# A fused linear-attention and mixture-of-experts block on one core: third slot reordered, x's deviations behind the gate steps, x1 squared in one operation

## The reference, cut to what matters

```
x = x + conv(_ln_c(x))            # layer norm over channels, then linear attention
    k = relu(Wk x + bk); q = relu(Wq x + bq); v = Wv x + bv      # 8 heads of 8 channels
    context = k^T v over all pixels of an image (per head)
    attended = context^T q;  conv = Wr attended + br
t = tokens(x)                      # one token of 64 channels per pixel
t = t + ffn(_ln_t(t))              # layer norm, then 8 experts, top 2 by a softmax router
    out = p1 * expert[i1](t) + p2 * expert[i2](t),  p normalised over the two
```

## Time and profile before

| | |
|---|---|
| median of 3 runs | 672.26 us (671.27 to 673.7) |
| the profiled execution's own time | 671.9 us |
| its span in the trace | 670.1 us |
| mean granted TensorE clock | 0.992 of full speed |
| PE busy | 616.2 us (92%), 8318 instructions |
| DVE busy | 515.1 us (77%), 1176 instructions |
| ACT busy | 425.2 us (63%), 832 instructions |
| POOL busy | 396.1 us (59%), 350 instructions |

### The profile page before, as it was taken

The page is one execution under the profiler, slowest core; times in us unless marked ns, Lnnn a source line. Parts: engine busy times, 40 slices in busy tenths (PEclk is TensorE's granted clock), DMA queues, the critical chain, the costliest instruction groups (busy, mean ns, idle before and its releaser), DMA issues.

```text
span 670.1 us, 21498 instructions
## 1 busy us (share of the span) xinstructions
PE 616.2 (92%) x8318; PEld 276.3 (41%) x8318; DVE 515.1 (77%) x1176; ACT 425.2 (63%) x832; POOL 396.1 (59%) x350
## 2 busy tenths in 40 slices
PE   3799989779999999999999999999999999998887
PEld 1566656444444444444444444444332332332222
DVE  3534455978888888889788787987799999989844
ACT  2355545576666675766757576766766776766642
POOL 7232342237565655666666556655577777777875
PEclk9799989999999999999999999999999999999999
DMA  6223635666555566655545665554565667446542
GB/s 149 56 76 79 146 97 129 150 167 159 122 122 134 126 147 146 159 142 138 133 111 130 147 152 127 129 116 104 133 154 127 157 172 170 101 111 142 126 111 48
DMA packets 32662, 86.21 MB, mean 129 GB/s; under 512 B 7650, under 2 KB 7826, under 8 KB 32562
## 3 DMA queue, kind: packets, MB, share of 16 engines
q1 hardware_dynamic: 32082, 84.64, 52.8%
q0 software_dynamic: 288, 0.19, 0.2%
q10 hardware_dynamic: 192, 0.01, 0.0%
HBM read 34.47 MB, written 16.78 MB: 76 GB/s over the span
## 4 chain that ended last, share of the span: by engine, by line
PE 62%; DVE 18%; ACT 10%; issue 7%; DMA 1%; POOL 1%; ACTq 0%; DVEq 0%; SPq 0%; POOLq 0%
PE bank L1092 26%; PE bank L1078 7%; PE bank L1015 5%; PE bank L993 4%; PE bank L979 4%; DVE z L826 3%; PE bank L938 3%; PE bank L1089 3%; PE bank L962 3%; DVE x L731 3%; ACT grows L569 2%; DVE xnT L686 2%; PE bank L1039 2%; DVE osb L836 2%; ACT L529 2%
## 5 line engine op out<-in xcount | busy, mean ns | idle before, releaser
L442 POOL TENSOR_TENSOR z<-gbs,x1d 128x512 f32<-128x512 f32 x256 | 320.2, 1275 | 185.2 <-ACT gbs L575 72.6
L1095 PE MATMUL bank<-z,ew 128*64 128x512 f32 x512 | 243.7, 598 | 0.0
L1092 PE MATMUL bank<-z,ew 128*64 128x512 f32 x512 | 243.6, 598 | 0.0
L826 DVE TENSOR_TENSOR z<-bank,x1d 128x512 f32<-128x512 f32 x256 | 164.7, 675 | 16.2 <-PE bank L1078 16.2
L575 ACT COPY gbs<-bank 128x512 f32<-128x512 f32 x256 | 140.7, 594 | 43.8 <-PE bank L1078 41.3
L433 POOL TENSOR_TENSOR xsq<-xin 128x512 f32<-128x512 f32 x64 | 65.4, 1043 | 81.7 <-DMA xin<-in_x_dram 76.0
L1078 PE MATMUL bank<-grows,sel 64*64 64x512 f16 x1024 | 93.2, 387 | 16.3 <-ACT grows L569 7.3
L1092 PEld LDWEIGHTS bank<-z,ew 128*64 128x64 f32 x512 | 64.9, 136 | 104.6 <-issue 96.3
L503 ACT COPY xn<-bank 128x512 f32<-128x512 f32 x64 | 34.4, 589 | 62.8 <-PE bank L938 62.8
L1095 PEld LDWEIGHTS bank<-z,ew 128*64 128x64 f32 x512 | 64.7, 136 | 0.0
L686 DVE TENSOR_TENSOR xnT<-bank,rstd 128x512 f32<-128x512 f32 x64 | 41.0, 682 | 30.2 <-PE bank L924 28.5
(11 more groups left out here) (135 smaller groups left out, 804.8 us busy)
## 6 DMA issues: line engine op xcount, KB each, us to landing
x1d<-x SPq DMA_DIRECT2D x128, 256.0 KB, 4.5
xin<-in_x_dram SPq DMA_DIRECT2D x64, 256.0 KB, 4.2
x_again<-in_x_dram SPq DMA_DIRECT2D x64, 256.0 KB, 4.2
out_dram<-osb SPq DMA_DIRECT2D x128, 128.0 KB, 2.4
k<-in_const_dram SPq DMA_DIRECT2D x1, 453.5 KB, 3.8
ew_nat<-in_L_ffn_expert_w_dram POOLq DMA_DIRECT2D x2, 64.0 KB, 6.4
sel<-in_const_sel_dram SPq DMA_DIRECT2D x1, 128.0 KB, 3.4
bk_rows<-bk_wide ACTq DMA_DIRECT2D x6, 1.0 KB, 1.7
```

What stands on the lines that cost most here:

```text
L442: pool.tensor_tensor(z[:, 1, i % R_Z, :], gbs[:, i % R_Z, :], x1d[:, g % 2, 1, u * NT:(u + 1) * NT], ALU.mult).then_inc(z_pool, 1)
L826: dve.tensor_tensor(z[:, 0, i % R_Z, :], bank[:, :], x1d[:, g % 2, 0, u * NT:(u + 1) * NT], ALU.mult).then_inc(taken_of(("spread", i, 0)), 1)
L1092: pe.matmul(out_bank[0:C, :], ew[:, j, :], z[:, 0, i % R_Z, :], start=False, stop=(j == PAIRS - 1), skip_group_check=True).then_inc(prod_d ...
L1095: pe.matmul(out_bank[C:P, :], ew[:, j, :], z[:, 1, i % R_Z, :], start=False, stop=(j == PAIRS - 1), skip_group_check=True).then_inc(prod_d ...
```

## The change

It does three things, in the lists of all engines concerned. In slot 2 the order of uses becomes spread(i), queries, attended, spread(i+1), on PE and on ACT, and in the list of bank uses. In slot 3 DVE runs x's last three deviation steps behind the gate steps instead of before them. ACT squares x1 in one operation of 1024 columns, which waits for both halves of x1, and the routing rows wait for one signal per group.

```diff
@@ bank_uses
             if k == 2:
+                for i in iterations(n, k + 1)[:1]:
+                    yield from (("spread", i, s) for s in range(S))
                 if real(n - L_KEYS):
                     yield from (("queries", n - L_KEYS, s) for s in range(S))
-                for i in iterations(n, k + 1)[:1]:
-                    yield from (("spread", i, s) for s in range(S))
                 if real(n - L_ATTEND):
                     yield from (("attended", n - L_ATTEND, u) for u in range(U))
@@ ACT
-            def square_x1(g, u):
-
-                when_taken(act, ("attended", g, u))
+            def square_x1(g):
+
+                for u in range(U):
+                    when_taken(act, ("attended", g, u))
                 if g:
                     when_filled(act, ("rows", g - 1 + L_ROUTE, 0))
-                nc.scalar.activation(x1sq[:, u * NT:(u + 1) * NT], x1[:, g % R_X1, u * NT:(u + 1) * NT], ACT.Square
-                                     ).then_inc(x1_squared, 1)
+                nc.scalar.activation(x1sq[:, :], x1[:, g % R_X1, :], ACT.Square).then_inc(x1_squared, 1)
...
                     if k == 2:
+                        for i in iterations(n, k + 1)[:1]:
+                            copy_gates(i)
                         if real(n - L_KEYS):
                             for s in range(S):
                                 take_queries(n - L_KEYS, s)
-                        for i in iterations(n, k + 1)[:1]:
-                            copy_gates(i)
...
                     if k == 3:
                         if real(n - L_ATTEND):
-                            for u in range(U):
-                                square_x1(n - L_ATTEND, u)
+                            square_x1(n - L_ATTEND)
@@ DVE
-                    if k == 3 and real(n - L_COLS):
-                        x_deviations(n - L_COLS, 4, N_XSTAT)
                     for phase, (k0, k1) in gates_by_phase.items():
                         if quad_in(n, k, phase) is not None:
                             gates(quad_in(n, k, phase), k0, k1)
+                    if k == 3 and real(n - L_COLS):
+                        x_deviations(n - L_COLS, 4, N_XSTAT)
                     for i in iterations(n, k + 1)[1 if k == 2 else 0:]:
                         product(i)
@@ PE
-                    pe.wait_ge(x1_squared, (g + 1) * U)
+                    pe.wait_ge(x1_squared, g + 1)
...
                     if k == 2:
+                        for i in iterations(n, k + 1)[:1]:
+                            broadcast(i)
                         if real(n - L_KEYS):
                             make_queries(n - L_KEYS)
-                        for i in iterations(n, k + 1)[:1]:
-                            broadcast(i)
                         if real(n - L_ATTEND):
                             attend(n - L_ATTEND)
```

## The result

The changed kernel is slower: 677.36 us median of 13 runs (676.29 to 678.86) against 673.03 us of the kernel before (13 runs, 671.27 to 676.08). The ratio is 1.0066, with a 95% interval of 1.0053 to 1.0079, so 3.6 to 5.3 us, under 1% of the time. The profiled execution took 676.59 us, its span is 674.8 us.

A forecast was written before the change was run, and what follows sets the result against it. PE, busy 92% of the span, was taken as the bound, with DVE a second bound in odd steps. Savings of 5.4 + 0.9 + 0 + 0.4 = 6.7 us from 671.9 gave 665.2 us; range 660 to 675.5.

The forecast's parts named there:

- Order of slot 2, even steps: Slot 2, eight even steps 18 to 32: PE waits 0.59 us instead of 1.27, saving 0.68 us each, 5.4 us.
- The wait for one gate copy: Slot 2, even steps: PE still waits 0.59 us for one gate copy, where it waited 1.27 for two queries.
- Order of slot 2, odd steps: Slot 2, odd steps 17 to 31: last spreading 0.46 us shorter each, 3.7 us in all, if DVE allows; counted as 0.
- the second bound: Odd steps: the chain runs on DVE without a pause; if DVE stays where it is, PE arrives earlier and waits.
- If L653 is through first, only L654 is stopped. I take this value.: Slot 3, odd steps: L654 stopped until 314.34, DVE's product at about 314.3 as before, so the odd steps give 0.
- the first rival: Slot 3, odd steps: POOL stops L653 and L654 in a row, 1.2 us in eight steps, +9.6, 674.8 us; chance 0.27.
- The pair of steps: An odd and an even step together: expected 0.7 us shorter, as a sign that the forecast holds.
- the one stop: Slot 3, odd steps: only one of x's deviation steps stopped, none in the even steps; 665.2 us, chance 0.43.
- Even steps, x's steps: Slot 3, even steps: x's deviation steps meet no stop, only the gates' own L652 does; PE keeps its 0.68 us.
- Squares: ACT's square of x1: one operation saves 0.1 us each; on the chain in steps 11 to 14, 0.4 us.
- In the expectations: Forecasts written for the follow-up runs; deviations alone: no odd-step stop, 2.2 us less than before, ratio 0.997.

## Why the prediction was wrong

The forecast was 665.2 us with 0.6 on faster; the kernel came out slower, outside the range. By its own steps:

- **Order of slot 2, even steps.** Right: 0.68 us each was forecast and 0.68 is measured (19.43 to 18.75), in the changed kernel and alone. The wait for one gate copy stayed, as forecast.
- **Order of slot 2, odd steps.** Right: the piece lost 0.5 us (0.46 was forecast), and gave nothing by itself, because DVE is the second bound there. The run with the order alone shows it.
- **The step that failed: "If L653 is through first, only L654 is stopped. I take this value."** The two instants were worked out as 313.08 for L653 and 313.07 for POOL, 8.00 and 7.99 us behind the slot's start. They came out as 316.56 - 308.57 = 7.99 and 316.52 - 308.57 = 7.95. The working was right to 0.04 us and still could not say who comes first. POOL did; L653 was stopped by the first product and L654 by the second (L652 and L653 in the changed kernel's lines), which is the first rival word for word. It was priced at 1.2 us in each of eight odd steps; measured is 19.92 - 18.73 = 1.19. The pair of steps, forecast 0.7 us shorter, is 0.5 us longer (38.16 to 38.67). Between steps 17 and 34 the rival's terms come to 9.6 - 5.4 - 0.5 = 3.7 us more than before, and 3.4 are measured. The rival's 674.8 us lies 2.6 us below the measured median and 1.8 us below the profiled execution. In that execution the stretch ahead of step 17 is 1.7 us longer, 1.1 of them at the lower clock; the remainder of the median is left open.
- **Why the one stop was taken.** A tie of 0.01 us between a gain and a loss was given to the gain, 0.43 against 0.27, with no row that spoke for it. The taken case exists: in the run with the deviations alone the second step began 0.09 us ahead of POOL's pair (316.44 and 316.53), was through in 0.17 us beside it, and only the third was stopped. Which of the two cases this kernel would be was beyond the working, so a hit would have been luck. And the range ended at 675.5, 0.7 above the centre of the rival, so the rival's own spread was cut off; the measured 677.36 is that case, with the remainder on top.
- **Even steps, x's steps.** Right: none is stopped, only the gates' own first step, 1.15 us. The margin was as thin as forecast: the last of x's steps ends at 298.51 and POOL's next pair starts at 298.59.
- **Squares.** 0.4 us less was forecast; alone they show no difference (1.0001, interval 0.9984 to 1.0018), which neither confirms nor refutes 0.4. The 0.1 us for each square is right (1.16 to 1.07); that the squares of steps 11 to 14 hold up the kernel is not shown.
- **In the expectations:** the run with the deviations alone was forecast at 0.997 and came out at 1.0074. The missed term is a wait that x's steps had covered: without the new order the gate steps wait 0.39 us for ACT's exponentials.

## What to carry to other kernels

Moving three steps of 0.2 us each cost more here than a whole slot's new order gained. Before moving small DVE operations, list which of them can be stopped beside POOL, and where POOL's instructions will stand after the rest of the change, since a gain elsewhere moves them too. Put such steps where a known idle stretch of POOL begins (here 1.65 us between two pairs), not where it ends; the three steps took 2.66 us across its end (316.41 to 319.07) and 0.58 us at its start (307.95 to 308.53). When the working says that two events tie, give both outcomes the same weight, let the range hold both with their spread, and look for the version in which they don't meet.

## What had not been expected of the hardware

A multiplication by a constant with one input and the output in SBUF, 16 elements wide, is stopped by POOL's product just as an operation with two inputs is (1.27 and 1.20 us in a row), while a reduction of the same size runs in 0.17 us. POOL's clearing of 256 columns (0.31 us) did not stop a DVE step with two inputs in SBUF (0.18 us). A stop lasted until the running POOL product was over, and where a second product followed without a gap it caught the next DVE step, though 0.04 us lay between: two steps of 0.17 us became 2.47 us. For a product that begins out of an idle stretch of POOL the edge lies within 0.13 us: a step that began 0.04 us behind the product's start was stopped (1.27 us, in eight odd steps of the changed kernel), one that began 0.09 us ahead of it was not (0.17 us, in eight odd steps of the run with the deviations alone).

The granted clock of TensorE from 136 to 144 us was 0.79 in the changed kernel's profile and 1.00 in that of the kernel before. In both, PE had just been idle for 3.3 us, waiting for ACT's low gate parts (PE timelines, the changed kernel, then the kernel before):

```profile
139.19 1.01 PE L1063 MATMUL bank<-eye,gT 128*128 128x128 f16 x8 [3.28 <-ACT gT L562]
```
```profile
138.86 0.61 PE L1064 MATMUL bank<-eye,gT 128*128 128x128 f16 x8 [3.27 <-ACT gT L562]
```

One execution fell to the lower of the two levels (1.2 GHz) for a few microseconds and the other did not. From 120 to 146 us the mean granted clock is 0.80 to 0.93 in eight of the ten profiles and 1.00 in two, the kernel before and the one with the deviations alone; and the mean over the whole execution ranges from 0.986 to 0.997 among the 23 executions of the kernel before that stand beside the first four runs. So such a drop in one profile is not to be put down to an edit.
